# The per-row channel mix as 64-row, 64-column matmuls on the two halves of the array, in a clamped low-rank linear kernel

## What is computed

```python
y = einsum('bct,bcd->bdt', x, cond_weights[itok])     # the mix: 64 x 64 per batch row
z = einsum('bsd,od->bso', y, W) + b                   # 1024 x 1024
u = einsum('bsd,edr->ebsr', y, A)                     # E*R = 8*16 = 128
m = einsum('ebsr,ero,e->bso', u, B, p_scores)
gamma = minimum(0.5 * norm(z) / (norm(m) + 1e-6), 1.0)
out = x + z + gamma * m
```

## Time and profile before

| | us |
|---|---|
| median of 3 runs | 1031.05 |
| lowest and highest run | 1029.73, 1031.88 |
| span of the profiled execution, first to last instruction | 1029.6 |

### The profile page before, as it was taken

One profiled execution on the slowest core, in us unless ns is written; L12 is line 12 of the kernel. 1 busy time (PEld: TensorE's weight loads), 2 busy tenths in 40 slices (PEclk: granted clock), 3 DMA queues, 4 the chain that ended last, 5 costly groups with the idle time before them and its releaser, 6 DMA issues.

```text
span 1029.6 us, 15207 instructions
## 1 busy us (share of the span) xinstructions
PE 1017.3 (99%) x5260; PEld 856.4 (83%) x5260; DVE 351.2 (34%) x620; ACT 289.2 (28%) x685; POOL 165.2 (16%) x263
## 2 busy tenths in 40 slices
PE   7999999999999999999999999999999999999997
PEld 5888888888888888888888888888888888888885
DVE  4433233233333332332333333323323333233332
ACT  5322223223223322232232232222322322222211
POOL 0211111111111111111111111111111111111112
PEclk9999999999999999999999999999999999999999
DMA  8112122121221211211212212112112122121111
GB/s 324 52 74 79 44 81 75 48 81 41 81 81 41 81 66 57 81 61 61 81 41 81 81 41 81 61 62 81 57 65 81 41 81 81 41 81 49 74 42 41
DMA packets 21367, 73.58 MB, mean 71 GB/s; under 512 B 2409, under 2 KB 3434, under 8 KB 21354
## 3 DMA queue, kind: packets, MB, share of 16 engines
q1 hardware_dynamic: 21354, 73.41, 19.6%
HBM read 39.85 MB, written 33.55 MB: 71 GB/s over the span
## 4 chain that ended last, share of the span: by engine, by line
PE 98%; DMA 1%; DVE 0%; ACT 0%; SPq 0%; issue 0%; DVEq 0%; POOLq 0%; POOL 0%; ACTq 0%
PE z_ps L439 70%; PE mix_ps L419 11%; PE m_ps L456 9%; PE u_ps L430 9%; DMA x_in<-in_x_dram 1%; DVE w_lo L327 0%; SPq L172 0%; ACT w_hi L241 0%; DVE rows L408 0%; DVE rows L368 0%; DVEq L59 0%; ACT squares L289 0%; POOLq L59 0%; ACT y_hi L245 0%; SPq L170 0%
## 5 line engine op out<-in xcount | busy, mean ns | idle before, releaser
L439 PE MATMUL z_ps<-w_hi,y_hi 128*128 128x512 f32 x1024 | 415.9, 406 | 2.2 <-DVE w_lo L327 2.2
L439 PE MATMUL z_ps<-w_hi,y_lo 128*128 128x512 f32 x1024 | 405.8, 396 | 0.0
L439 PE MATMUL z_ps<-w_lo,y_hi 128*128 128x512 f32 x1024 | 405.4, 396 | 0.0
L289 ACT ACTIVATE squares<-rows 128x512 bf16<-128x512 f32 x128 | 80.8, 631 | 628.2 <-DVE rows L368 536.8
L439 PEld LDWEIGHTS z_ps<-w_hi,y_lo 128*128 128x128 f32 x1024 | 192.7, 188 | 46.3
L439 PEld LDWEIGHTS z_ps<-w_hi,y_hi 128*128 128x128 f32 x1024 | 193.4, 189 | 43.0 <-ACT y_hi L245 2.4
L439 PEld LDWEIGHTS z_ps<-w_lo,y_hi 128*128 128x128 f32 x1024 | 193.4, 189 | 40.9
L368 DVE TENSOR_TENSOR rows<-z_ps,bias 128x512 f32<-128x512 f32 x128 | 88.6, 692 | 365.7 <-PE z_ps L439 365.7
L333 DVE TENSOR_TENSOR y_lo<-mix_ps,y_hi 128x512 fp32r<-128x512 f32 x128 | 88.2, 689 | 232.7 <-ACT y_hi L245 232.5
L224 POOL TENSOR_TENSOR rows<-rows,x_in 128x512 f32<-128x512 f32 x64 | 81.7, 1277 | 428.0 <-DVE rows L368 428.0
L419 PEld LDWEIGHTS mix_ps<-mixer,x_in 128*128 128x128 f32 x1024 | 131.3, 191 | 10.8 <-DMA x_in<-in_x_dram 2.3
(11 more groups left out here) (38 smaller groups left out, 479.8 us busy)
## 6 DMA issues: line engine op xcount, KB each, us to landing
x_in<-in_x_dram SPq DMA_DIRECT2D x64, 512.0 KB, 3.3
out_dram<-rows SPq DMA_DIRECT2D x63, 512.0 KB, 2.7
rows<-in_L_ffn_W_dram SPq DMA_DIRECT2D x4, 512.0 KB, 7.4
w_late<-in_L_ffn_W_dram SPq DMA_DIRECT2D x4, 512.0 KB, 11.0
cond_all<-in_L_cond_weights_dram SPq DMA_DIRECT2D x2, 256.0 KB, 4.0
a_in<-in_L_ffn_A_dram SPq DMA_DIRECT2D x1, 512.0 KB, 14.3
bm_in<-in_L_ffn_B_dram SPq DMA_DIRECT2D x1, 512.0 KB, 8.9
bias<-in_L_ffn_b_dram SPq DMA_DIRECT2D x1, 512.0 KB, 9.2
```

Of the source, the lines that this page charges most:

```text
L289: nc.scalar.activation(squares[:, cols], z_b[:, j % 2, cols], ACT.Square, accum_out=z_sq[:, j % 2, h:h + 1]).then_inc(z_squared, 1)
L439: summed = nc.tensor.matmul(z_ps[h][:, :], left[:, g, k, r], right[:, k, h * H:(h + 1) * H], start=(k == 0 and n == 0), stop=(k == KC - 1 ...
```

## The change

The mixer loses its zeros: it becomes `[P, 2, 64]`, the two matrices one above the other. A block of the mix is now two matmuls, one for each batch row q: stationary is the block's 128 columns of the 64 rows of `x_in` that belong to q, and the 64 columns of q's matrix stream. Rows 0 to 63 of the array serve q = 0, rows 64 to 127 q = 1. The results of q go to the bank `mix_ps[q]`, all 8 blocks side by side with 64 columns each; a split handles one batch row, in 8 pieces of 64 columns. The mix of a tile is no longer in two halves: `mix(j)` is one run of 16 fp32 matmuls, ahead of `linear(j, 0)` (and of `down(0)` at the start), and both its splits stand together, ahead of `square_z(0)` on ScalarE and of `add_bias(0)` on VectorE. At the start both splits of tile 0 stand ahead of the first split of `w`.

```diff
-        mixer = sb("mixer", [P, 2, P], fp32)
+        mixer = sb("mixer", [P, 2, C], fp32)
...
-            nc.gpsimd.memset(mixer[:, :, :], 0.0).then_inc(mixer_zeroed, 1)
...
-            def split_y(j, h):
-                nc.scalar.copy(y_hi[:, j // 2 % 2, h * HC:(h + 1) * HC, j % 2 * P:(j % 2 + 1) * P],
-                               mix_ps[h][:, :].rearrange("p (k n) -> p k n", k=HC)).then_inc(y_hi_ready, 1)
+            def split_y(j, q):
+                tokens = slice(j % 2 * P + q * C, j % 2 * P + (q + 1) * C)
+                nc.scalar.copy(y_hi[:, j // 2 % 2, :, tokens],
+                               mix_ps[q][:, :].rearrange("p (k n) -> p k n", k=KC)).then_inc(y_hi_ready, 1)
...
-                    made = nc.scalar.copy(mixer[part, j % 2, q * C:(q + 1) * C],
+                    made = nc.scalar.copy(mixer[part, j % 2, :],
...
+            for q in range(PER):
+                act.wait_ge(mix_done, q + 1)
+                split_y(0, q)
             for k in range(KC):
-                if k < 2:
-                    act.wait_ge(mix_done, k + 1)
-                    split_y(0, k)
                 split_w(k)
...
                     if not opening and (not last or j + 2 < BODY):
-                        act.wait_ge(mix_done, 2 * t + 5)
-                        split_y(j + 2, 0)
+                        for q in range(PER):
+                            act.wait_ge(mix_done, 2 * t + 5 + q)
+                            split_y(j + 2, q)
...
-                    if not last or j + 2 < BODY:
-                        act.wait_ge(mix_done, 2 * t + 6)
-                        split_y(j + 2, 1)
                     square_z(1)
...
-            def mix(j, h):
-                for k in range(HC):
-                    mixed = nc.tensor.matmul(mix_ps[h][:, k * P:(k + 1) * P],
-                                             x_in[:, j % BODY, (h * HC + k) * P:(h * HC + k + 1) * P],
-                                             mixer[:, j % 2, :], start=True, stop=True)
-                mixed.then_inc(mix_done, 1)
+            def mix(j):
+                for k in range(KC):
+                    for q in range(PER):
+                        part = slice(q * C, (q + 1) * C)
+                        mixed = nc.tensor.matmul(mix_ps[q][:, k * C:(k + 1) * C],
+                                                 x_in[part, j % BODY, k * P:(k + 1) * P],
+                                                 mixer[part, j % 2, :], start=True, stop=True)
+                        if k == KC - 1:
+                            mixed.then_inc(mix_done, 1)
...
+            pe.wait_ge(y_hi_ready, 2)
+            pe.wait_ge(y_lo_ready, 2)
             for k in range(KC):
-                if k % HC == 0:
-                    pe.wait_ge(y_hi_ready, k // HC + 1)
-                    pe.wait_ge(y_lo_ready, k // HC + 1)
...
-            pe.wait_ge(y_lo_ready, 3)
-            mix(2, 0)
             pe.wait_ge(y_hi_ready, 4)
             pe.wait_ge(y_lo_ready, 4)
+            mix(2)
             pe.wait_ge(a_hi_ready, 1)
             pe.wait_ge(a_lo_ready, 1)
             down(0)
-            mix(2, 1)
...
                         pe.wait_ge(mixer_ready, t + 3)
-                        pe.wait_ge(y_lo_ready, 2 * t + 3)
-                        mix(j + 2, 0)
+                        pe.wait_ge(y_lo_ready, 2 * t + 4)
+                        mix(j + 2)
                     pe.wait_ge(z_b_ready, 2 * t - 1)
                     linear(j, 0)
...
                     up(j)
-                    if not last or j + 2 < BODY:
-                        pe.wait_ge(y_lo_ready, 2 * t + 4)
-                        mix(j + 2, 1)
                     pe.wait_ge(z_b_ready, 2 * t)
                     linear(j, 1)
```

More of the change, by code:

```diff
@@ L109, in conditioned_clamped_low_rank_linear_kernel @@
         w_in = [rows[:, k, :] if k < 4 else w_late[:, k - 4, :] for k in range(KC)]
-        mix_ps = [pb(f"mix_ps{h}", [P, H]) for h in range(2)]
+        mix_ps = [pb(f"mix_ps{q}", [P, H]) for q in range(PER)]
         z_ps = [pb(f"z_ps{h}", [P, H]) for h in range(2)]
@@ L328, in split_w, with split_y @@
                                         ALU.subtract).then_inc(w_lo_ready, 1)
-            def split_y(j, h):
-                part = (slice(None), j // 2 % 2, slice(h * HC, (h + 1) * HC), slice(j % 2 * P, (j % 2 + 1) * P))
-                nc.vector.tensor_tensor(y_lo[part], mix_ps[h][:, :].rearrange("p (k n) -> p k n", k=HC),
+            def split_y(j, q):
+                part = (slice(None), j // 2 % 2, slice(0, KC), slice(j % 2 * P + q * C, j % 2 * P + (q + 1) * C))
+                nc.vector.tensor_tensor(y_lo[part], mix_ps[q][:, :].rearrange("p (k n) -> p k n", k=KC),
                                         y_hi[part].bitcast(fp32), ALU.subtract).then_inc(y_lo_ready, 1)
+            for q in range(PER):
+                dve.wait_ge(y_hi_ready, q + 1)
+                split_y(0, q)
             for k in range(KC):
-                if k < 2:
-                    dve.wait_ge(y_hi_ready, k + 1)
-                    split_y(0, k)
                 split_w(k)
@@ L372, in step @@
                     if opening:
-                        dve.wait_ge(y_hi_ready, 5)
-                        split_y(2, 0)
+                        for q in range(PER):
+                            dve.wait_ge(y_hi_ready, 5 + q)
+                            split_y(2, q)
                     if j % 2 == 0:
@@ L379, in step @@
                     if not opening and (not last or j + 2 < BODY):
-                        dve.wait_ge(y_hi_ready, 2 * t + 5)
-                        split_y(j + 2, 0)
+                        for q in range(PER):
+                            dve.wait_ge(y_hi_ready, 2 * t + 5 + q)
+                            split_y(j + 2, q)
                     add_bias(0)
-                    if not last or j + 2 < BODY:
-                        dve.wait_ge(y_hi_ready, 2 * t + 6)
-                        split_y(j + 2, 1)
                     dve.wait_ge(norm_m_ready, t + 1)
@@ L463, in _ @@
             pe.wait_ge(mixer_ready, 1)
-            for h in range(2):
-                mix(0, h)
+            mix(0)
+            pe.wait_ge(y_hi_ready, 2)
+            pe.wait_ge(y_lo_ready, 2)
             for k in range(KC):
-                if k % HC == 0:
-                    pe.wait_ge(y_hi_ready, k // HC + 1)
-                    pe.wait_ge(y_lo_ready, k // HC + 1)
                 pe.wait_ge(w_hi_ready, k + 1)
@@ L480, in _ @@
                     pe.wait_ge(mixer_ready, 2)
-                    for h in range(2):
-                        mix(1, h)
+                    mix(1)
             pe.wait_ge(x_loaded[2], 16)
             pe.wait_ge(mixer_ready, 3)
-            pe.wait_ge(y_lo_ready, 3)
-            mix(2, 0)
             pe.wait_ge(y_hi_ready, 4)
             pe.wait_ge(y_lo_ready, 4)
+            mix(2)
             pe.wait_ge(a_hi_ready, 1)
```

6 lines of the change are left out of this document (2 added, 4 removed).

## The result

The changed kernel takes 1055.89 us in the median (1055.18 to 1057.40), the kernel before 1031.14: a ratio of 1.0241, 95% interval 1.0226 to 1.0255. It is slower by 24.8 us where 113 had been forecast. The sign was right and the time lies in the range, but the term that carried the forecast was wrong by a factor of five.

What follows compares the result with a forecast made beforehand. TensorE, busy 99%, was taken as the bound. Span 1029.6 + 111.0 (mix) + 1.1 + 0.9 (opening) = 1142.6; with the median 1.45 above the profiled span, 1144 us, range 1029 to 1165.

Steps and rivals of the forecast that it cites:

- the term that carried the forecast: The mix on TensorE: 32 load-and-matmul pairs a tile, one after the other, adding 111.0 us.
- What bounds the kernel, and what sets the 0.111 us: TensorE, busy 99%, bounds; in the mix, weight loads and streamed columns balance at 0.111 us a matmul.
- The mix, part by part: Cost of the half-array mix: between 0.89 and 3.52 us a tile; 225.3 us chosen for the run, +111.0.
- one path at 0.110: Mix loads into half the rows cost full price and follow one another: 3.52 us a tile, chance 0.37.
- rival 1: Mix loads and matmuls of the two array halves run side by side: 1029.3 to 1033.5 us, chance 0.19.
- The code's order helps an overlap little: In the mix, two pairs on one half, then two on the other, were expected to overlap little; no size of its own.
- rival 2: Mix halves side by side with a loss, 1050 to 1121 us, chance 0.25; first form: array empties at shape changes, +34.7.
- The second form: In the mix, a load can't go under its own half's columns: +53.6 us, 1087 with the opening.
- rival 4: Half-price mix loads, chance 0.12: side by side 976 us (fast part); on one path about 1033 (slow part, 0.03).
- The opening: Lost cover at the start: z later by 1.1 us, and u's way bare ahead of up(0), 0.9 us.
- The half clock: Another half-speed clock stretch in the first 40 us would cost some 1.6 us; counted as nothing, left to the range.
- The loop: Moved waits, splits and copies in the steady loop stay hidden, with no TensorE wait for y_lo: 0 us.

Runs made afterwards that it cites:

- e3: The changed kernel with each mix matmul streaming 32 of its 64 columns; 1054.9 us.
- e4: The changed kernel with each mix load bringing 96 of its 128 columns; 1028.4 us.
- e5: The changed kernel plus one spare full-array fp32 matmul in the middle of linear(j, 1) of tiles 1 to 63; 1070.4 us.
- e10: Block-diagonal mix on all 128 rows in the changed kernel's order, each matmul cut in two by its loaded columns (64 each); 1053.6 us.
- e8: The changed kernel with mix blocks taken two of batch row 0, then two of row 1, and so on; 1059.5 us.
- e2: The changed kernel with the mix's loops exchanged: all 8 blocks of batch row 0, then all 8 of row 1; 1199.1 us.
- e1: The changed kernel's order of work, but with the block-diagonal 128x128 full-array mix of the kernel before; 1033.77 us.
- e9: The changed kernel with each half matmul cut into two 64-row, 64-column pieces, plus a bf16 carrier matmul for the wait ahead of each mix in the steps; 1005.1 us.
- e11: e9 without the carrier matmul, its waits ahead of linear(j, 1)'s last chunk, and tile 3's mix between down(0) and up(0); 1001.61 us.

## Why the prediction failed, step by step

**What bounds the kernel, and what sets the 0.111 us**: right. TensorE stayed the bound, and load and columns balance at 0.11; e3, e4, e5 and e10 each show one side of it.

**"The mix, part by part"**: this is the step that failed. I took both bounds right (3.52 and 0.89 us a tile) and chose the upper, "one path at 0.110", because the rows "show loads strictly one after the other". But all loads of the kernel before need all rows of the array (128x128), so each had to wait for the one before it: the rows could not have shown two loads at a time. They spoke for neither case, and I read the absence as evidence. The one row that did bear on it, a matmul that left the queue 0.03 us after its load began, I put down to rival 1 and gave it less weight than it had. "The code's order helps an overlap little" was wrong as well: two pairs of one half, then two of the other, overlap in full, and four and four all but 0.05 us a tile (e8); only long runs don't (e2). The term measured: 16 x 0.111 + 0.34, 2.12 us a tile instead of 3.52, so +22 us instead of +111. That 1056 lies inside 1029 to 1165 is no merit of this term: by it alone the time was 1140 to 1148, and the range reached lower only because it took in rival 1.

**The rivals**: it was rival 2 in its first form, side by side with a loss at the change of shape, at a chance of 0.25 for both of its forms; rival 1 alone, with its 0.19, had the mechanism of the slots. Its price was put at 34.7 us (two tails of 0.163 and two bare loads of 0.108 a tile, 0.54) and was 22 (0.35): the load of the new shape goes 0.085 to 0.09 us after the last columns (506.49 to 506.58), not 0.163, and the last half matmul streams for half as long. The second form (a load can't go under its own half's columns) would have made slots of 0.164 and falls with the rows above; rival 4 (a cheaper load in half of the rows) falls in its fast part with the slots of 0.111. Its slow part, half-priced loads on one path at 0.056 each, would have given the same slots in the changed kernel, in e3 and in e4, and with the excursions the same 1056; it falls with the paired starts and with e2, where loads on one half stand 0.111 apart. It had 0.03.

By its slots the trace bears out the Trainium skill's rule in "TensorEngine Tiling (Array Packing)", section "Key Properties", that different tiles load weights and run matmuls in parallel: 32 half loads in the time of 16 full ones, and 64 quarter loads in 1.02 us. The other rule of the Trainium skill there, that a change of the tiling mode drains TensorE, agrees too, at 0.35 us for the way there and back. And the Trainium skill's rule in "TensorE: Matmul & The Clock Gate", section "LDWEIGHTS (loading the stationary operand)", that a load's time goes by its columns, holds for 64 rows: slots of 0.111, 0.085 and 0.058 us for 128, 96 and 64 columns.

**The opening**: right. +2.0 forecast, +2.8 measured in e1 (1.6 to 3.6). Its two places are as forecast: z later by 0.9 in e1 (forecast 1.1), and TensorE idle 1.01 ahead of up(0) (forecast 0.9). In the changed kernel itself, whose first mix is longer, z starts at 14.07 (forecast 15.1 with a mix of 3.52 us). The half clock was left to the range; in the profiled execution of the changed kernel it lasted longer than before, in its first 40 us:

```profile
0.00:40.00 40.00, 32.45 (x220) 24.61 (x221) 17.65 (x22) 18.45 (x32) 2.60 (x8) 0.87 0.58 211
```

0.87 against 0.96: another 0.09 x 40 = 3.6 us of full clock. My estimate of the part on the path is 1.5 us, the 3 of the opening less the 1.5 by which e1's span, at 0.96, lies over that of the kernel before.

**The loop**: right. No wait of TensorE for y_lo appears, and e1 leaves no room for one (932.2 us against 932.3 from up(1) to up(60)).

## What to carry to other kernels

Where a trace can't show an overlap, because every instruction in it needs the whole resource, its rows price the resource and say nothing on whether two halves of it work side by side. Small fp32 matmuls on a cut-up array are priced by the slower of the load (by its columns) and the stream, per piece; cutting the rows alone leaves a load-bound mix where it was, cutting the loaded columns with them halves it, and each change between full and cut array and back costs 0.35 us (0.31 with column halves), so it wants few and long excursions. Give the pieces turns of a few matmuls, not long runs.

## What the runs showed that I had not expected

- The time of the changed kernel can't tell half-priced loads on one path from full-priced loads side by side: both give slots of 0.111 us. The paired starts in the trace and the long runs on one half (e2) tell them apart.
- Four quarter pieces load and stream side by side: 64 fp32 load-and-matmul pairs in 16 slots of some 0.058 us (e9), although the code issues the two pairs of a piece one behind the other.
- The overlap reaches over runs of four pairs (e8, 0.05 us a tile lost) but not over runs of 16 (e2, four slots of 16 overlap).
- With matmuls on one half of the rows at a time for most of a mix's 3.4 us, the granted clock went down to the 1.2 GHz level again and again (mean 0.944), with TensorE busy 99% of the span (e2). With both halves at work it stayed at 1.00 all through the loop, in the changed kernel and in e3 to e11. What in the one-half work brings the fall is open.
